# Spreading the dense products over all heads of a trip, and steps of a recurrence over four trips

## The reference, cut to what matters

```python
# layer 0: x = x + attention(x)
q_word, k_word, v_word = jnp.split(x @ c_attn_w + c_attn_b, 3, axis=-1)
k_img, v_img = img @ uk_w.T + uk_b, img @ uv_w.T + uv_b      # one more key and value
scores = where(kj <= qi + 1, q @ k.T / sqrt(32), -10000) + mask
x = x + (softmax(scores) @ v) @ c_proj_w + c_proj_b
# layer 1: x = x + hs
xw = x @ Wx + b
def step(prev_h, xw_t):
    next_h = jnp.tanh(prev_h @ Wh + xw_t)
    return next_h, next_h
```

## Time and profile before

| | before |
|---|---|
| median of 3 runs | 1851.33 us (1847.14 to 1851.88) |
| profiled execution | 1850.24 us |
| its span | 1848.5 us |
| TensorE clock granted, mean | 0.948 |
| PE busy | 1657.4 us (90%) |
| LDWEIGHTS busy | 1389.1 us (75%) |
| DVE busy / ACT busy | 889.7 us (48%) / 708.1 us (38%) |
| DMA, mean | 120 GB/s |

### The profile page before, as it was taken

One profiled execution on the slowest core, in us unless ns is written; L12 is line 12 of the kernel. 1 busy time (PEld: TensorE's weight loads), 2 busy tenths in 40 slices (PEclk: granted clock), 3 DMA queues, 4 the chain that ended last, 5 costly groups with the idle time before them and its releaser, 6 DMA issues.

```text
span 1848.5 us, 67862 instructions
## 1 busy us (share of the span) xinstructions
PE 1657.4 (90%) x29292; PEld 1389.1 (75%) x29292; DVE 889.7 (48%) x2986; ACT 708.1 (38%) x2205; POOL 149.4 (8%) x248
## 2 busy tenths in 40 slices
PE   3788888989898998989899998989999887999997
PEld 2777777878787887878787886878778666888875
DVE  4254345454555454655645555556656563222222
ACT  2254444444443444444444444444444442111110
POOL 1001000000000000001011000001000000000000
PEclk7879888999999999999999998999999999999998
DMA  6455346444445355565555456566656640100000
GB/s 233 143 149 157 114 139 170 127 131 120 122 118 135 103 134 129 139 141 137 150 138 148 116 136 151 140 161 157 159 145 161 137 111 25 27 15 17 26 15 20
DMA packets 228442, 221.67 MB, mean 120 GB/s; under 512 B 22952, under 2 KB 187048, under 8 KB 227632
## 3 DMA queue, kind: packets, MB, share of 16 engines
q1 hardware_dynamic: 211568, 175.86, 36.7%
q0 software_dynamic: 16576, 41.46, 8.0%
HBM read 141.45 MB, written 75.76 MB: 118 GB/s over the span
## 4 chain that ended last, share of the span: by engine, by line
PE 72%; DMA 9%; DVE 8%; issue 5%; ACT 4%; SPq 3%; POOL 0%; DVEq 0%; POOLq 0%; ACTq 0%
PE rec L924 22%; PE turned L847 8%; PE dense L380 7%; DMA kq<-kq_dram 6%; PE dense L381 6%; PE dense L382 6%; PE dense L895 5%; PE scores L839 4%; PE pv L860 4%; PE scores L924 3%; DVE pre L751 3%; PE pv L878 2%; ACT hist L593 2%; DVE probs L687 1%; SPq L427 1%
## 5 line engine op out<-in xcount | busy, mean ns | idle before, releaser
L924 PE MATMUL rec<-wh,hist 128*8 128x128 f32 x14336 | 487.9, 277 | 29.7 <-ACT hist L593 23.3
L924 PEld LDWEIGHTS rec<-wh,hist 128*8 128x8 f32 x14336 | 356.2, 94 | 112.6 <-ACT hist L593 66.1
L551 ACT ACTIVATE probs<-probs,nmax 128x128 f32<-128x128 f32 (+3 forms) x512 | 287.2, 561 | 187.2 <-DVE nmax L687 179.6
L593 ACT ACTIVATE hist<-pre 128x32 f32<-128x32 f32 x512 | 131.7, 257 | 573.4 <-DVE pre L761 331.9
L687 DVE CUSTOM_DVE_ANT_0 probs<-scores,msk,nimg 128x128 f32<-128x128 f32 (+3 forms) x512 | 276.2, 545 | 131.2 <-PE scores L839 128.6
L839 PE MATMUL scores<-kq 96*128 96x128 f32 (+3 forms) x512 | 212.5, 420 | 82.6 <-DMA kq<-kq_dram 81.0
L751 DVE STREAM_TRANSPOSE pre<-rec 128x128 f32<-128x128 f32 x448 | 141.4, 316 | 295.6 <-PE rec L924 292.2
L847 PE MATMUL turned<-ident,probs 128*128 128x128 f32 x1280 | 250.0, 296 | 1.4 <-DVE probsT L696 1.0
L847 PEld LDWEIGHTS turned<-ident,probs 128*128 128x128 f32 x1280 | 150.3, 145 | 69.2 <-issue 56.7
L839 PEld LDWEIGHTS scores<-kq 96*128 96x128 f32 x512 | 107.7, 211 | 109.5 <-DMA kq<-kq_dram 86.8
L696 DVE COPY probsT<-turned 128x128 f32<-128x128 f32 (+3 forms) x256 | 124.8, 487 | 112.2 <-PE turned L847 111.6
(11 more groups left out here) (119 smaller groups left out, 2291.1 us busy)
## 6 DMA issues: line engine op xcount, KB each, us to landing
kq<-kq_dram SPq DMA_DIRECT2D x96, 320.0 KB, 5.7
kq<-kq_dram SPq DMA_DIRECT2D x96, 256.0 KB, 4.8
kq<-kq_dram SPq DMA_DIRECT2D x96, 192.0 KB, 3.7
kq_dram<-qs_hi SPq DMA_DIRECT2D x128, 128.0 KB, 2.1
kq_dram<-ks_hi SPq DMA_DIRECT2D x128, 128.0 KB, 3.2
kq<-kq_dram SPq DMA_DIRECT2D x96, 128.0 KB, 2.6
xin<-x SPq DMA_DIRECT2D x32, 256.0 KB, 3.1
kq_dram<-qs_lo SPq DMA_DIRECT2D x64, 128.0 KB, 2.4
```

What stands on the lines that cost most here:

```text
L551: act.activation(probs[:, g % PROBS, 0:n], probs[:, g % PROBS, 0:n], ACT.Exp, scale=-1.0, bias=nmax[:, e, h:h + 1], accum_out=rowsum[:, e, ...
L593: act.activation(hist[:, g // HALF % 2, :, :, g % HALF], pre[:, :, 0:B], ACT.Tanh).then_inc(h_ready, 1)
L924: last = pe.matmul(d[Q * j:Q * j + B, 0:P], hist[:, before // HALF, f, :, before % HALF], wh[:, f, P * j:P * j + P], start=f == 0 and not ...
```

## The change

The same instructions are issued, but in another order, in three parts.

**Dense.** `project` and its rule for h < 10 go. Trip g now carries at h = 0 to 8, one a unit: v parts 0 and 1, the store of sequence 0's values, q and k of chunk 3 with its imgscore, v parts 2 and 3, the store of sequence 1's values; all these are of trip g itself. From h = 10 to 31 it carries `finish(g-1)` and chunks 0 to 2 of trip g+1, with the split of x (`xsplit`) put in between the second and the third `wx`. Before the first head only chunks 0 to 2 of trip 0 are done. A load is put in the list as soon as the chunk that it reads is there, not only at the end of a unit, and SP's lag of `kqload` goes from 0.0 to 1.4. The values have a semaphore for each sequence instead of one, and the shift of each fourth head waits for its own chunk's imgscore.

**Steps.** All 128 steps of a block lie evenly by weight between `finished` of its last trip and the first `wx` three trips on (that is the wx which ends the fourth window of before). One rule is added: before the first `wx` of trip 4(b+1)+r, all steps up to 32(r+1) must have been placed; those that are behind are placed there together.

**Values' products.** Where no step is next to a `pv`, the nearest one within three events is moved right before or behind it. Weights of several events are changed as well.

```diff
-    "SP": {"xload": 0.8, "vimgload": 0.5, "q": 1.3, "k": 1.3, "kqload": 0.0, "vload": 0.5},
+    "SP": {"xload": 0.8, "vimgload": 0.9, "q": 1.3, "k": 1.3, "kqload": 1.4, "vload": 0.5},
...
-    def project(g):
-        return ([("xsplit", g, k, 0.0) for k in range(2)]
-                + [e for c in (0, 1) for e in (("q", g, c, 1.4), ("k", g, c, 1.4), ("imgscore", g, c, 0.5))]
-                + [("v", g, i, 1.4) for i in range(4)] + [("vstore", g, 0, 0.0)]
-                + [e for c in (2, 3) for e in (("q", g, c, 1.4), ("k", g, c, 1.4), ("imgscore", g, c, 0.5))])
+    def chunk(g, c):
+        return [("q", g, c, 1.5), ("k", g, c, 1.5), ("imgscore", g, c, 0.5)]
+
+    def values(g, e):
+        return [("v", g, 2 * e, 1.5), ("v", g, 2 * e + 1, 1.5), ("vstore", g, e, 0.0)]
...
+        return ([("proj", g, c, 1.5) for c in range(C)] + [("xload", g + 2, 0, 0.0)] * (g + 2 < TRIPS)
+                + [("x1n", g, e, 0.55) for e in range(2)]
+                + [(last, g, c, 1.8 * (last == "wx")) for c in range(C)] + [("finished", g, 0, 0.0)])
...
+            side, until = values(g, 0) + chunk(g, 3) + values(g, 1), 9
+        if h == 10:
+            side, until = [], UNITS - 1
+            if 0 < g <= TRIPS:
+                side += finish(g - 1)
+            if g + 1 < TRIPS:
+                at = max(len(side) - 3, 0)
+                side[at:at] = begin(g + 1)
+                side += chunk(g + 1, 0) + chunk(g + 1, 1) + chunk(g + 1, 2)
...
+            emit([("pv", v, 0, 0.1 + 0.213 * (block_of(v // 8) + 1))])
...
+            emit([("turn", v, 0, 0.05 + 0.11 * (block_of(v // UNITS) + 1))])
...
+            emit([("score", u, 0, max(0.11, 0.053 * (block_of(g) + 1)) + 0.1)])
...
+        take = len(side) if g >= TRIPS or h >= until else -(-len(side) // (until + 1 - h))
...
-    for group in range((BLOCKS - 1) * PAIRS):
-        first, last = ends[group + PAIRS - 1] + 1, begins[group + PAIRS]
+    for b in range(BLOCKS - 1):
+        first, last = ends[(b + 1) * PAIRS - 1] + 1, begins[(b + 2) * PAIRS - 1]
...
-            while n < STEPS and done >= whole * (n + 0.5) / STEPS:
-                place.setdefault(at, []).append(group * STEPS + n)
+            while n < P and (done >= whole * (n + 0.5) / P
+                             or at + 1 == begins.get((b + 1) * PAIRS + n // STEPS)):
+                place.setdefault(at, []).append(b * P + n)
...
+    for m, (kind, *_) in enumerate(main):
+        if kind == "pv":
+            near = [at for at in (m - 1, m, m - 2, m + 1, m - 3, m + 2) if at in place]
+            if near and near[0] not in (m - 1, m):
+                at = m - 1 if near[0] < m else m
+                steps = place[near[0]]
+                place[at] = [steps.pop() if near[0] < m else steps.pop(0)]
...
-                    sp.wait_ge(v_stored, 32 * (trip + 1))
+                    sp.wait_ge(v_stored[e], 16 * (trip + 1))
...
-                    for n in range(4):
-                        wait_copied(pool, "v", g, n)
-                    for e in range(2):
-                        pool.dma_start(v_dram[2 * r + e, P * p:P * p + P, :], vnew[:, e, :]).then_inc(v_stored, 16)
+                    for n in range(2):
+                        wait_copied(pool, "v", g, 2 * i + n)
+                    pool.dma_start(v_dram[2 * r + i, P * p:P * p + P, :], vnew[:, i, :]).then_inc(v_stored[i], 16)
```

More of the change, by code:

```diff
@@ L61, in main_order @@
 def main_order():
-    out = []
-    def project(g):
-        return ([("xsplit", g, k, 0.0) for k in range(2)]
-                + [e for c in (0, 1) for e in (("q", g, c, 1.4), ("k", g, c, 1.4), ("imgscore", g, c, 0.5))]
-                + [("v", g, i, 1.4) for i in range(4)] + [("vstore", g, 0, 0.0)]
-                + [e for c in (2, 3) for e in (("q", g, c, 1.4), ("k", g, c, 1.4), ("imgscore", g, c, 0.5))])
+    out, seen, loads = [], set(), [("kqload", group, 0, 0.0) for group in range(TILES)]
@@ new lines, in main_order, with emit @@
+    loads += [("vload", group, 0, 0.0) for group in range(VTILES)]
+    def emit(events):
+        for event in events:
+            out.append(event)
+            seen.add(event[:3])
+            for load in list(loads):
+                trip, k = divmod(load[1], 8)
+                if (("k", trip, k % C) if load[0] == "kqload" else ("vstore", trip, k // C)) in seen:
+                    out.append(load)
+                    loads.remove(load)
+    def chunk(g, c):
+        return [("q", g, c, 1.5), ("k", g, c, 1.5), ("imgscore", g, c, 0.5)]
@@ L71, in finish, with begin @@
+    def values(g, e):
+        return [("v", g, 2 * e, 1.5), ("v", g, 2 * e + 1, 1.5), ("vstore", g, e, 0.0)]
+    def begin(g):
+        return [("xsplit", g, k, 0.0) for k in range(2)]
     def finish(g):
         last = "keep" if block_of(g) == BLOCKS - 1 else "wx"
-        return ([("proj", g, c, 1.4) for c in range(C)] + [("xload", g + 2, 0, 0.0)] * (g + 2 < TRIPS)
-                + [("x1n", g, e, 0.85) for e in range(2)]
-                + [(last, g, c, 1.7 * (last == "wx")) for c in range(C)] + [("finished", g, 0, 0.0)])
@@ L92, in main_order @@
+    emit([("xload", 0, 0, 0.0), ("xload", 1, 0, 0.0), ("mskload", 0, 0, 0.0), ("mskload", 0, 1, 0.0),
+          ("vimgload", 0, 0, 0.0), ("vimgload", 0, 1, 0.0)] + begin(0) + chunk(0, 0) + chunk(0, 1) + chunk(0, 2))
+    side, until = [], 0
     for u in range(HEADS + 2 * H):
         g, h = divmod(u, UNITS)
+        block, h2 = divmod(u, H)
         if h == 0 and g < TRIPS:
[L95 to L99, removed]
@@ L100, in main_order @@
-        block, h2 = divmod(u, H)
+            side, until = values(g, 0) + chunk(g, 3) + values(g, 1), 9
[7 more added lines that the diff above has]
+                side += chunk(g + 1, 0) + chunk(g + 1, 1) + chunk(g + 1, 2)
         if h2 == 8 and 0 < block <= 2 * TRIPS:
-            out.append(("norm", block - 1, 0, 0.9))
+            emit([("norm", block - 1, 0, 0.9)])
@@ L103, in main_order @@
             if block + 1 < 2 * TRIPS:
-                out.append(("vimgload", (block + 1) // 2, (block + 1) % 2, 0.0))
+                emit([("vimgload", (block + 1) // 2, (block + 1) % 2, 0.0)])
         if h2 == 9 and 0 < block <= 2 * TRIPS:
-            out.append(("attnlow", block - 1, 0, 0.0))
-        p = block_of(min(g, TRIPS - 1))
+            emit([("attnlow", block - 1, 0, 0.0)])
         if u >= PV_LAG and (u - PV_LAG) % HC == 0 and u - PV_LAG < HEADS:
[L109 to L112, removed]
+            v = (u - PV_LAG) // HC
@@ L113, in main_order @@
+            if v + VTILES < GROUPS:
+                loads.append(("vload", v + VTILES, 0, 0.0))
+            emit([("pv", v, 0, 0.1 + 0.213 * (block_of(v // 8) + 1))])
         if TURN_LAG <= u < HEADS + TURN_LAG:
             v = u - TURN_LAG
-            out.append(("turn", v, 0, 0.11 * (block_of(v // UNITS) + 1)))
+            emit([("turn", v, 0, 0.05 + 0.11 * (block_of(v // UNITS) + 1))])
         if u < HEADS:
-            out.append(("score", u, 0, max(0.11, 0.053 * (p + 1)) + 0.06))
             if u % HC == HC - 1 and u // HC + TILES < GROUPS:
@@ L119, in main_order @@
                 loads.append(("kqload", u // HC + TILES, 0, 0.0))
+            emit([("score", u, 0, max(0.11, 0.053 * (block_of(g) + 1)) + 0.1)])
             if h2 == 15 and block + 2 < 2 * TRIPS:
-                out.append(("mskload", (block + 2) // 2, block % 2, 0.0))
+                emit([("mskload", (block + 2) // 2, block % 2, 0.0)])
         if 0 < block <= 2 * TRIPS:
-            out += {1: [("imgprob", block - 1, 0, 0.0)], 2: [("total", block - 1, 0, 0.0)],
-                    4: [("imgturn", block - 1, 0, 0.15)], 5: [("rowturn", block - 1, 0, 0.45)]}.get(h2, [])
@@ L125, in main_order @@
[L125 to L136, removed]
+            emit({1: [("imgprob", block - 1, 0, 0.0)], 2: [("total", block - 1, 0, 0.0)],
+                  4: [("imgturn", block - 1, 0, 0.15)], 5: [("rowturn", block - 1, 0, 0.5)]}.get(h2, []))
@@ L137, in main_order @@
+        take = len(side) if g >= TRIPS or h >= until else -(-len(side) // (until + 1 - h))
+        emit(side[:take])
+        side = side[take:]
     return out
@@ L154, in order @@
             done += main[at][3]
-            while n < STEPS and done >= whole * (n + 0.5) / STEPS:
-                place.setdefault(at, []).append(group * STEPS + n)
+            while n < P and (done >= whole * (n + 0.5) / P
+                             or at + 1 == begins.get((b + 1) * PAIRS + n // STEPS)):
+                place.setdefault(at, []).append(b * P + n)
                 n += 1
-        assert n == STEPS
+        assert n == P
+    for m, (kind, *_) in enumerate(main):
[5 more added lines that the diff above has]
+                place[at] = [steps.pop() if near[0] < m else steps.pop(0)]
+                if not steps:
+                    del place[near[0]]
     plan = {name: [] for name in ("PE", "DVE", "ACT", "POOL", "SP")}
@@ L171, in step @@
     def step(t):
-        put("step", t, 0, 0.85)
```

(19 more changed lines are left out.)

## The result

The changed kernel takes 1801.6 us (median of 4; 1793.3 to 1803.8) against 1849.2 us; the ratio is 0.9735, 95% interval 0.9697 to 0.9772. It is 48 us faster, where 104 were forecast, and lies just above the stated range. The direction was right; less than half of the gain came.

A forecast was written before the change was run, and what follows sets the result against it. PE, busy for 90%, was taken as the bound, with order mattering through its waits and clock. Terms -64 -37 -3 -8 -10 -7 +25 gave -104 from 1850.2, so 1746 us; range 1716 to 1795.

The forecast's parts named there:

- part 8: DVE's extra waits, shorter units from h = 10 and vload behind the values' store: nothing, but near; 0 to 40 us.
- Part 1, the fifth head: PE's load waits before each trip's fifth head: v parts and q placed ahead fill them, 64 us gone.
- Part 2, the clock: PE's low clock in block 0 and twelve further trips: dense work everywhere holds it up, 37 us gone.
- Part 3, the start: PE's wait for the first load, now right behind the store of chunk 0: 3 us gone.
- Part 4, the last steps: Waits for the state in the last group of steps, most now placed earlier: 8 us gone.
- Part 5, the joins: Values' products next to steps save switches between 32-row strips and the rest: 34 x 0.29, 10 us gone.
- Part 6, the split: The split of x now lies between wx products, not right ahead of the q needing it: 7 us gone.
- Part 7, the heaps: Steps forced together before the first wx, in heaps of 6, 4 and 3: 25 us added.
- Rival C: Heaped steps take 2.5 us each and the clock falls at the two largest: 27 us more, 1773; chance 0.16.
- Rivals B: The wait moves to the ninth head, as SP stands at vload: 54 us back, 1800; chance 0.13.
- D: SP's single list makes each load group late, by 1.1 us: slower, 1875 with the clock; chance 0.05.
- The sign that the size fails: Mean clock of 84:308 stays near 0.88 if block 0's low clock comes from small heads, not missing dense work.

The follow-up runs named there:

- first run: The changed kernel with one number changed, POOL's lag of the mask load from 0.0 to 2.6, so the x1n store goes ahead of it: 1743.6 us, ratio 0.9436.
- after: The changed kernel itself, with all three parts of the change, against the kernel before: 1801.6 us, ratio 0.9735.
- the run with more work: The kernel before with 12 more products ahead of the scores of heads 1, 2 and 3 in each trip but the first: 1814.7 us, ratio 0.9814.
- The recurrence part alone: The kernel before with the changed kernel's steps and joins, dense products and lags as before: 1835.2 us, ratio 0.9922.
- The run without the joins: The changed kernel with later mask load and no heaps, without moving steps next to the values' products: 1731.0 us, ratio 0.9369.

## Why the prediction was wrong

The step that failed is part 8, "At nothing". It looked at what the later store of the values meets behind POOL's mask load, and priced that right (no wait before a ninth head but 1.4 us in trip 0). It did not ask the same of the other store in that list. x1n moves from heads 12 and 13 to 14 and 15; who is ahead of it in POOL's list, and who reads or writes x1nat next, were not followed. The price was 58 us (first run against after), and 1746 was forecast where the kernel without that wait measures 1743.6. The agreement is partly luck, as the other terms show:

- *Part 1, the fifth head*: 64 us forecast; 74.6 became 7.3 us. Right.
- *Part 2, the clock*: 37 us. The mechanism is shown by the run with more work. In after, low time fell only from 54 + 87 us (0.88 and 0.96 over 84:308 and 308:1400) to 45 + 66, because new waits take the place of the old; with the mask load moved it is 18 + 22, 101 us of low time less, which at the 0.40 of the earlier trace rows is 40 us. In after it is 30 us less, worth 12.
- *Part 3, the start*: 3 us forecast for the first load, whose wait went from 6.33 to 1.37 us. The lag of vimgload, 14 us in the order of before, had no term. Part of it was given back: with short units in trip 0, PE waits 4.3 us for chunk 3's load before head 12 of trip 0.
- *Part 4, the last steps*: 8 us; the waits for hist of the earlier trace rows, 10.4 us, are 1.4 us in the same part of after. Right. The recurrence part alone gave 14 us for the 11 of parts 4, 5 and the pairs, but other waits moved in it too.
- *Part 5, the joins*: 34 new ones forecast, 18 made (66 to 84 in the programs' order), as 77 of the pv have a step next to them and not nearly all 96: behind a heap there is none within three events. The run without the joins gives 4 us for 17 of them; not separated from nothing.
- *Part 6, the split*: 7 us; the row is gone. Right, though the new wait for xw (6.9 us) eats as much.
- *Part 7, the heaps*: 25 us forecast; heaps of 6, 4 and 3 are there, and their removal gives 17 us with the mask load moved, 20 without.
- *Part 8*: nothing forecast, 58 us measured.

So with the mask load moved the start gave more than forecast, the joins less, the heaps cost less, and the new wait for xw stood against them; that the sum came within 3 us is luck in these terms, and not in the mechanism of parts 1 and 2.

Rival C had the low clock at a heap right (0.54 over 801:816), not its share of the time. Rivals B and D did not happen: no such wait before ninth heads, and 7.3 us for the loads in all. Of the signs of being right, the fifth heads (1.2 us at most), the waits for kq and the heaps of 6, 4 and 3 came; three others did not. The waits for hist were 56.9 us and not near 35, the mean clock from 400 to 1500 us was 0.97 and not 0.99, and the steps in a heap stood 2.87 us apart at the low clock. The sign that the size fails, a mean near 0.88 in 84:308, nearly came (0.90), but not for the reason given there, the small heads: with the mask load moved the same stretch has 0.96, so the waits at x1nat in trips 1 to 4 held it down.

Not tried: kqload with its old lag of 0.0 in the new order, and a second buffer for the row sums, which would take the wait of x1nat away at its root instead of by order.

## What to carry to other kernels

When work moves in an order that several in-order queues share, walk every instruction that it issues through its queue, stores included: find what now stands ahead of it, and which later write waits for its landing. A lag or sort key of a load that blocks its queue is a term of its own; two such numbers were worth 14 and 58 us here, where the whole change gained 48. And count a wait of PE with what the clock costs behind it, also when you only move the wait.

## What the runs showed of the hardware that was not expected

- Adding 540 products of 256 columns made the kernel 34 us faster, by filling waits that drop the clock from 2.4 to 1.2 GHz.
- Six steps in a row, with PE waiting 0.97 us of each 2.04, brought the clock down during the heap itself; a step then took 1.90 instead of 1.07 us and the interval grew to 2.87 us. Single gaps of that size between other products, as the 0.97 us ahead of 1550.87 in the earlier trace rows, stood at full clock.
- A mask load of 256 KB took 6.6 us of POOL's time beyond its issue, since POOL waited for it in order. With the store ahead of it POOL waited 5.7 us for it all the same (at 1199.5 in the first run), and DVE's waits for the store were 4.0 us instead of 44.0.
